# 16-dim attention heads in one block: projection, stacking, scores, exp times V, sums and output, with a lag of two head pairs

## The reference, cut to what matters

```
q, k, v = split into 16 heads of 16 features of   xq @ Wq, xk @ Wk, xk @ Wv
sim     = q @ k^T * scale          (causal: only keys up to the query)
e       = exp(sim - max over keys of sim)
out     = (e @ v) / (sum over keys of e)
x       = x + concat(out) @ Wo
```

## Time and profile before

| | |
|---|---|
| median of 3 runs | 4298.7 us (4296.89 to 4308.47) |
| the profiled execution | 4299.54 us, span 4297.7 us from first to last instruction |
| TensorE busy | 3401.4 us, 79% of the span |
| VectorE busy | 2078.9 us, 48% |
| ScalarE busy | 1146.9 us, 27% |
| mean granted TensorE clock | 0.888 of full speed |
| 12 executions of the three blocks | first at 93.7 us, last ends at 4162.7 us |

### The profile page before, as it was taken

How to read it: one execution, slowest core, us unless ns; L and a number is a source line. 1 busy time by engine, 2 the same in 40 slices (tenths; PEclk the granted TensorE clock), 3 DMA queues, 4 the chain that set the end, 5 groups by cost and what they waited for, 6 DMA issues and landing times. The chain is left out here.

```text
span 4297.7 us, 49457 instructions
## 1 busy us (share of the span) xinstructions
PE 3401.4 (79%) x18289; PEld 2170.2 (50%) x18289; DVE 2078.9 (48%) x4553; ACT 1146.9 (27%) x2199; POOL 401.3 (9%) x381
## 2 busy tenths in 40 slices
PE   4778689678869967887986778798595888877888
PEld 3364555436455544645454455544593454454545
DVE  3655445465545546555555654554113435344353
ACT  1413125141223414122341312243131213112121
POOL 0010101010010101001010100101102000010100
PEclk9888899888889978898997979899797998989989
DMA  4000100200010010001001000100682110102011
GB/s 163 13 13 21 63 11 1 86 13 13 21 63 11 17 70 13 13 20 63 11 28 59 13 13 23 61 10 33 246 306 97 51 41 7 78 8 84 8 51 38
DMA packets 53212, 209.27 MB, mean 49 GB/s; under 512 B 4977, under 2 KB 37617, under 8 KB 41329
## 3 DMA queue, kind: packets, MB, share of 16 engines
q1 hardware_dynamic: 48128, 198.85, 12.5%
q0 software_dynamic: 1536, 4.20, 0.3%
q10 hardware_dynamic: 3312, 3.02, 0.2%
HBM read 186.89 MB, written 19.16 MB: 48 GB/s over the span
## 5 line engine op out<-in xcount | busy, mean ns | idle before, releaser
L643 DVE TENSOR_REDUCE nmax<-psum 128x1 f32<-128x512 f32 (+3 forms) x768 | 392.2, 553 | 135.6 <-PE psum L579 91.5
L685 ACT ACTIVATE probs<-psum 128x1024 f32<-128x1024 f32 (+3 forms) x384 | 304.4, 814 | 431.0 <-PE psum L607 290.0
L108 PE MATMUL psum<-select 128*128 128x512 f32 x1016 | 280.2, 431 | 82.9 <-PEq L120 82.9
L574 PE MATMUL psum<-ks,qs 64*128 64x512 f32 (+3 forms) x768 | 211.1, 546 | 139.5 <-DVE nmax L643 123.5
L108 PEld LDWEIGHTS psum<-select 128*128 128x128 f32 x1016 | 205.3, 208 | 156.9 <-issue 113.3
L316 ACT ACTIVATE xc<-psum 128x256 f32<-128x256 f32 x152 | 54.5, 389 | 790.1 <-PE psum L309 790.1
L265 POOL TENSOR_SCALAR rstd<-mean_var 128x4 f32<-128x4 f32 x48 | 10.9, 228 | 2491.5 <-DVE mean_var L290 2491.5
L574 PEld LDWEIGHTS psum<-ks,qs 64*128 64x128 f32 x768 | 89.0, 227 | 290.2 <-DVE nmax L643 269.5
L1490 ACT ACTIVATE exps<-exps,nmax 128x512 f32<-128x512 f32 x256 | 183.4, 717 | 71.4 <-DVE nmax L1436 71.0
L1436 DVE CUSTOM_DVE_ANT_0 exps<-psum,mrows 128x512 f32<-128x512 f32 x256 | 166.1, 689 | 67.9 <-PE psum L1383 64.6
L602 PE MATMUL psum<-qs,ks 64*128 64x512 f32 (+3 forms) x768 | 165.0, 435 | 7.8 <-ACT probs L685 7.8
(11 more groups left out here) (371 smaller groups left out, 6700.9 us busy)
## 6 DMA issues: line engine op xcount, KB each, us to landing
arena<-in_w SPq DMA_DIRECT2D x23, 1028.0 KB, 5.0
arena<-in_w SPq DMA_DIRECT2D x23, 1024.0 KB, 5.2
arena<-in_pack_L_ffn SPq DMA_DIRECT2D x4, 5184.5 KB, 15.5
arena<-in_pack_L_xattn SPq DMA_DIRECT2D x4, 4744.0 KB, 13.9
arena<-in_pack_L_ffn SPq DMA_DIRECT2D x4, 4120.0 KB, 13.1
arena<-in_pack_L_attn SPq DMA_DIRECT2D x5, 2432.0 KB, 9.2
arena<-in_pack_L_attn SPq DMA_DIRECT2D x9, 1280.0 KB, 5.5
arena<-ternary SPq DMA_DIRECT2D x4, 2056.0 KB, 7.8
```

The source lines that it names most:

```text
L108: pe.matmul(self.psum[:, bank, :], self.select[:, 0, :], self.select[:, 0:BANK // P, :], start=True, stop=True)
L574: mm = pe.matmul(net.psum[:, bank_of(s + j), 0:w], qs[half, p, qt * P:(qt + 1) * P], ks[half, p, 0:w], start=True, stop=not causal)
L643: dve.tensor_reduce(nmax[:, p, qt, n % 2:n % 2 + 1], net.psum[:, bank_of(s), 0:w], AX.X, ALU.max, negate=True).then_inc(row_read, 1)
L685: act.activation(probs[:, n % buffers, :, lo:T], net.psum[:, first:first + 2, lo:T], ACT.Exp, scale=scale)\
```

## The change

`stack_pairs` and `heads_of_four` are gone; `softmax_heads` is one block that also does the division and output of its sublayer.

- TensorE: the projections come first, then the stacking of pairs 0 and 1, then the score steps. The stacking of pairs 2 to 7 and the four value products stand between the score steps of pairs 0 and 1.
- ScalarE copies both q and k of the stacked pairs (k with ones as a bias) and all values; VectorE copies none of them any more.
- The lag is two pairs in place of three. Each pair's exp is done for all four key tiles in turn, so a `weigh`, which needs both pairs of a group, comes in four steps in a row and then not for four steps; the even pair's exp is kept in four tiles, the odd pair's in two.
- The division goes by groups of four heads: `totals` (four products with 4 columns) puts the sums on query rows, VectorE takes a reciprocal of 128x16 and widens it to 128x512, `spread_inverse` turns it back, VectorE scales o in place, `project` adds to the output. Groups 0 to 2 stand in the last eight steps beside the last exps, group 3 comes at the end.
- Semaphores per block 28 in place of 20. No DMA is added, removed or moved.

```diff
-SEMS = 20
+SEMS = 28
...
+    lag, steps = 2, NT
+    ring = (0, 1, 2)
...
+                def stack(p):
+                    for is_k in range(2):
+                        m, src = 2 * p + is_k, 2 * (p // 4) + is_k
+                        pe.wait_ge(high_done, src + 1)
+                        pe.wait_ge(low_done, max(src, min(m, 3)) + 1)
+                        if m >= 4:
+                            pe.wait_ge(stacked, m - 3)
...
+                def values(t):
+                    if t:
+                        pe.wait_ge(v_copied, t)
...
                 def row_scores(p, qt):
 
+                    if qt == 0:
+                        pe.wait_ge(stacked, 2 * p + 2)
...
                 def col_scores(n):
+                    p, kt = divmod(n, steps)
+                    if kt == 0:
+                        pe.wait_ge(row_read, put_slot(p) + 1)
                     if n >= 2:
                         pe.wait_ge(probs_done, n - 1)
+                    else:
+                        pe.wait_ge(stacked, outputs)
...
+                def totals(g):
+                    pe.wait_ge(o_done, g + 1)
+                    if g:
+                        pe.wait_ge(scaled, g)
+                    else:
+                        pe.wait_ge(row_read, turns)
+                    for t in range(NT):
+                        mm = pe.matmul(net.psum[:, 0, 4 * t:4 * t + 4], o[:, g, t * P:(t + 1) * P], net.gather[:, 0:PITCH:8],
+                                       start=True, stop=True)
+                    mm.then_inc(totals_done, 1)
+
+                def spread_inverse(g):
+                    pe.wait_ge(widened, g + 1)
...
+                def project(g):
+                    pe.wait_ge(scaled, g + 1)
...
+                stack(0)
+                stack(1)
                 for p in range(PAIRS + lag):
                     for i in range(steps):
                         if p < PAIRS:
                             row_scores(p, i)
+                        if p < 2:
+                            if i % 2 == 0:
+                                stack(2 + 3 * p + i // 2)
+                            else:
+                                values(2 * p + i // 2)
+                            if i == 3:
+                                stack(4 + 3 * p)
                         if p >= lag:
                             n = (p - lag) * steps + i
                             col_scores(n)
-                            if n % 2 and n >= 3:
-                                weigh((n - 3) // 2)
+                            last_p, last_kt = divmod(n - 1, steps)
+                            if n and last_p % 2:
+                                weigh(last_p // 2, last_kt)
                         if 1 <= p <= PAIRS and i == (PUT_AT // 2 - 1 if p < PAIRS else 0):
                             put(p - 1)
+                        if p >= PAIRS:
+                            at = (p - PAIRS) * steps + i
+                            if at in (1, 3, 5):
+                                totals(at // 2)
+                            if at in (2, 4, 6):
+                                spread_inverse(at // 2 - 1)
+                            if at in (3, 5, 7):
+                                project(at // 2 - 1)
+                weigh(GROUPS - 1, steps - 1)
+                totals(GROUPS - 1)
+                spread_inverse(GROUPS - 1)
+                project(GROUPS - 1)
...
+                        act.activation((ks if is_k else qs)[:, p, :], net.psum[:, 3 + m % 4, :], ACT.Identity, **bias).then_inc(stacked, 1)
...
+                    dve.reciprocal(inverse[:, g % 2, :, :], net.psum[:, 0, 0:NT * 4].rearrange("p (t h) -> p t h", t=NT)).then_inc(inverse_done, 1)
```

More of the change, by code:

```diff
@@ L530, in heads_of_four, with jobs @@
-def heads_of_four(net, qs, ks, v, o, scale, guard=None, causal=False):
-    lag, buffers = 3, 4
-    steps, units = NT, PAIRS // 2
-    tiles = 2 * NT
-    ring = (0, 1, 7)
     halves = [slice(j * STACK, (j + 1) * STACK) for j in range(2)]
+    if jobs is None:
+        def jobs(j, c):
+            return chunk_terms(*((W["wk"], ksrc) if j else (W["wq"], qsrc)), c), None
+    table = [jobs(j, c) for c in range(NC) for j in range(2)]
     def slot(p, n):
@@ L553, in heads_of_four @@
         with net.block() as (block, sem):
+            product_done, value_done, high_done, low_done = sem("product"), sem("value"), sem("high"), sem("low")
+            cos_done, sin_done, zeroed = sem("times cosine"), sem("times sine"), sem("zeroed")
+            placed, stacked = sem("parts in place"), sem("stacked q or k copied")
+            v_done, v_copied = sem("values product"), sem("values copied")
             cleared, scores_done = sem("spread zeroed"), sem("a tile's scores, both heads")
@@ L561, in _ @@
+            widened = sem("1/sum of a group, for each partition of a head")
+            spread_done, scaled, out_done = sem("1/sum on the heads' partitions"), sem("group scaled"), sem("output of a tile")
             @block.gpsimd
@@ new lines, in _ @@
+                for n, groups in enumerate(table):
+                    if rope and n >= 2:
+                        pe.wait_ge(sin_done, n - 1)
+                    for which, group in enumerate(groups):
+                        for where, lhsT, rhs, start, stop, turn in group or ():
+                            mm = pe.matmul(net.psum[:, job_bank(n, which), :], lhsT, rhs, start=start, stop=stop)
+                    mm.then_inc(product_done, 1)
+                stack(0)
+                stack(1)
@@ new lines, in _ @@
+                for n in range(len(table)):
+                    act.wait_ge(value_done if rope else product_done, n + 1)
+                    act.activation(high[:, n, :], source(n), ACT.Identity).then_inc(high_done, 1)
+                copy_stack(0)
+                copy_stack(1)
+                for p in range(2):
+                    for i in range(steps):
+                        if i % 2 == 0:
+                            copy_stack(2 + 3 * p + i // 2)
+                        else:
+                            copy_values(2 * p + i // 2)
+                        if i == 3:
+                            copy_stack(4 + 3 * p)
@@ new lines, in _ @@
+                for n in range(PAIRS * steps):
+                    p, kt = divmod(n, steps)
+                    lo = kt * P if causal else 0
+                    act.wait_ge(colscores_done, n + 1)
+                    if p % 2 and kt >= 2:
+                        act.wait_ge(pv_done, p // 2 * steps + kt - 1)
+                    if p >= 2:
+                        act.wait_ge(pv_done, (p // 2 - 1) * steps + (kt + 1 if p % 2 == 0 else steps))
+                    first = 3 + 2 * (n % 2)
+                    act.activation(probs(n)[:, :, lo:T], net.psum[:, first:first + 2, lo:T], ACT.Exp, scale=scale).then_inc(probs_done, 1)
```

229 lines of the change are left out of this document (91 added, 138 removed).

## The result

The change makes the kernel 0.7% faster: 4268.14 us in the median of 4 runs (4267.12 to 4270.88), before 4297.8 beside it; ratio 0.9931, 95% interval 0.9914 to 0.9948. The gain is 30 us where 164 were forecast; 4268 lies far outside the range of 4088 to 4212.

A forecast was written before the change was run, and what follows sets the result against it. No engine fills the span; each stage has its own bound, with VectorE busy 47.6 of 54.1 us in L0_xattn's rows. Gains of 13.8, 11.8 and 15.6 us, four times each, make 165: 4134 us, range 4088 to 4212.

The forecast's parts named there:

- three signs of being wrong: Row scores in pairs 0 and 1 wait for stacked copies; clock in pairs 2 to 7 below 0.9; a tail longer.
- Part 1, the head: First product to first maximum: gains of 10.5 us in L0_xattn, 10.3 in L1_attn, 14.1 in L3_attn per execution.
- Part 2, the rows: First to last maximum: L0_xattn gains 2.1 us less 2.0 for one clock fall, net 0.1; causal rows gain 0.
- A stack: Rows, pairs 0 and 1: a stacking product is four TensorE passes at 0.22 us, 0.9 in all.
- a value tile: Rows, pairs 0 and 1: a value product costs TensorE 0.86 us.
- the 2.0 taken: L0_xattn rows: price in us of one clock fall, counted in the middle steps of pair 2.
- The rival of falls in every even pair: L0_xattn rows: three clock falls of 2.0 us per execution, 72 less the 8 counted, 4198 us; chance 0.15.
- the same count gives less than 1 us either way: Causal rows: mask products fill the steps, so gain taken as 0, bounds 2 us up and down.
- Part 3, the tail: Last maximum to last add: 27.7 us against 30.9 in L0_xattn, gain 3.2; causal 26.3 against 27.8, gain 1.5.
- TensorE's queue to 19.2 us: L0_xattn tail: 2.3 to the add, 15.9 of queued TensorE products, 1.0 of uncovered VectorE answers.
- The serial end: L0_xattn tail, after 19.2 us: last group's product, copy, totals, reciprocal, spread, scaling, project and adds, ending at 27.7.
- my rivals: Falls in every even pair 4198 us (0.15); stacking waits 4242 (0.10); slower 4418 (0.03); better about 4100 (0.10).

The follow-up runs named there:

- the run with the old division: The changed kernel with division and output done by the block of before, after the block; head, rows and lag of two pairs stay: 4204.5 us.
- the old order: The kernel before with only its head changed, so order, lag of three pairs and division as before: 4189.6 us, 4190.6 in a second set.
- experiment 6: Two kernels with new head and division of before: order of before with lag three, 4189.6 us; the change's order with lag three, 4283.9 us.
- Run 3: The changed kernel with output products of groups 0 to 2 moved behind the last product of exp and v: 4205.7 us.
- Run 2: The changed kernel plus unread products in the tail: two ahead of each of the last eight column scores, sixteen at the end: 4262.4 us.
- experiment 7: Changed kernel with division of before and lag two, plus either values ahead of stacking, 4245.3 us, or two unread products before each of the last eight column scores, 4224.1.
- experiment 4: The changed kernel with late output products, plus two unread products ahead of each of the last eight column scores: 4203.2 us.
- the old order with late output: Order of before in the rows behind the new head, division by groups in the block, all output products late: 4172.6 us against 4297.8 before.

## Why the prediction was wrong

The sign was right and the size was not. Of the three signs of being wrong the last came true: the causal tails are longer than before. Of the 133 us that are missing (165 against 32 in the span), 71 are the tails, 36 the rows, 14 the code outside and 11 the heads.

**Part 1, the head: right but for the clock.** 12.6, 9.8 and 21.3 us were measured in the mean, 11.4, 9.9 and 19.5 forecast. The two that are longer than forecast have a clock below 1.00 in them (0.76 in the first L0_xattn, 0.93 in the last L3_attn). In the run with the old division two L3_attn heads stand at 1.00 and take 20.1.

**Part 2, the rows: two terms too small, one left out.** In the first L1_attn's pair 1, with TensorE's queue full:

```profile
330.61 0.50 PE L505 MATMUL psum<-high,select 128*128 128x512 f32 x1
...
331.75 0.38 PE L526 MATMUL psum<-ks,qs 64*128 64x256 f32 x2
...
332.19 1.13 PE L513 MATMUL psum<-arena,xc 128*128 128x256 f32 x4
...
333.25 0.44 PE L526 MATMUL psum<-ks,qs 64*128 64x384 f32 x2
```

A stack takes 1.14 from start to next start (330.61 to 331.75; forecast 0.9), a value tile 1.06 (332.19 to 333.25; forecast 0.86). In L0_xattn pairs 0 and 1 take 6.48 and 7.63 (5.95 and 6.6 forecast); the odd pairs' 6.97 and even pairs' 6.33 are close to 6.9 and 6.15. One pair in each L0_xattn holds a fall: 8.33 in place of 6.97, a price of 1.4 against the 2.0 taken. That it is one, as counted, is luck: it was counted in the middle steps of pair 2, and it comes in pair 5 or 7, among the products of exp and v. The rival of falls in every even pair, with the rule of the Trainium skill ("TensorE: Matmul & The Clock Gate", "psum-queue depth-cycling") beside it, did not come about in the rows. What failed is the sentence that in the causal rows "the same count gives less than 1 us either way". Maxima are shorter there (VectorE busy 34.6 of 51.1), so the stacks, values and bunched products are not beside anything longer. Pairs 0 and 1 take 13.7 from the first maximum, where before they took 11.5 to 12.1. Pairs 5 and 6 of the first L1_attn, the change ahead and the old order of experiment 6 behind:

```profile
356.00:362.69 6.69, 6.33 (x78) 3.16 (x76) 4.41 (x11) 2.82 (x4) 0.00 (x0) 1.00 0.01 2
362.69:368.07 5.38, 4.35 (x62) 2.85 (x60) 4.41 (x11) 3.29 (x5) 0.00 (x0) 1.00 0.00 0
```

```profile
353.42:358.96 5.54, 5.11 (x64) 2.65 (x62) 4.41 (x11) 4.14 (x5) 0.00 (x0) 1.00 0.01 4
358.96:364.93 5.97, 5.52 (x76) 3.31 (x76) 4.50 (x11) 1.96 (x4) 0.00 (x0) 1.00 0.00 0
```

At full clock and with the same work (TensorE busy 10.7 and 10.6 us in the two pairs) the bunched order takes 12.07 and the old one 11.51: TensorE fills the odd pair and has 1.0 us to spare in the even one. Behind the new head the old order takes back 22 of the rows' 36 us (experiment 6).

**Part 3, the tail: the clock taken as full, one product misplaced.** For L0_xattn I summed TensorE's queue to 19.2 us up to the last exp; it came at 19.1. The agreement is partly luck: the sum holds a third output product (1.73) and a third product of exp and v (1.0), which TensorE ran behind the last column scores (181.17), and leaves out the 1.56 us from these scores to the end of the last exp and 0.1 of each column score and spread. The serial end, forecast at 8.45, took 11.6:

```profile
181.17 0.50 PE L554 MATMUL psum<-qs,ks 64*128 64x512 f32 x2
...
181.71 1.02 ACT L745 ACTIVATE probs_odd<-psum 128x1024 f32<-128x1024 f32 x1 [1.49 <-PE psum L554]
...
182.59 1.99 PE L599 MATMUL psum<-arena,o 128*128 128x256 f32 x8
184.52 0.62 PE L573 MATMUL psum<-probs_even,v 128*32 128x512 f32 x2
...
190.11 3.45 PE L599 MATMUL psum<-arena,o 128*128 128x256 f32 x8 [0.78 <-DVE o L699]
```

The last exp ends at 182.73, but its product with v waits to 184.52 behind the output product of group 2: 1.8. The last output product runs at 1.2 GHz, 3.45 for 1.95: 1.5. Run 3 undoes the first and finds 26.7 us at full clock, 1.0 under my 27.7. In the causal tails, forecast at 26.3, nearly all of the miss is the clock. Run 2 at full clock and in the change's own order has 31.1 with 32 products too many. The sixteen in the first half are worth 2.9 (experiment 7), the sixteen at the end 1.1: what follows the last exp takes 10.8 with them, and 9.7 in the change's second L3_attn tail, whose end stands at 1.00. So some 27 would be left (an estimate), 7 less than L1_attn's 34.3 and close to the forecast. The order is 3.5 of these 27 (experiment 4), but that cost was in the forecast's queue too. The two are not independent: run 3 has the first fall where it was in all causal tails, but not the second, and no fall in three of the four L0_xattn tails. The step that failed is the clock, which Part 3 took at full speed throughout. That it could fall in the tail was in none of my rivals; I looked for falls in the rows alone, because the tail before stood at 1.00.

**Outside.** The code outside the twelve executions took 3049.0 us of the span before, 3062.9 after, and 3052 to 3064 in the profiles of the other runs. Two of the 14 us are seen ahead of the first L0_xattn, which starts at 95.6 us in place of 93.7, with a fall of the clock from 71.0 us on that the trace of before has not. Another 11 lie in the three stretches from the end of an L1_attn to the next L0_xattn, which took 419.4, 416.7 and 415.9 us before and 421.3, 421.0 and 420.9 after, with mean clocks of 0.91 to 0.92 and 0.90. What sets such falls in stages that the change doesn't touch was not tried and stays open.

## What to carry over

Before moving work beside other work, ask of each stage which engine sets its pace: beside VectorE's long maxima two thirds of the values' cost were hidden, beside the shorter causal ones half. In an in-order queue, put nothing that is needed only at the end ahead of what another engine waits for; moving three groups of output products behind the last product of exp and v was worth 62 us and costs no work; at full clock on both sides it brings the last exp 3.4 to 3.5 us sooner in each execution, and the rest came with the clock. And where a change puts other products into a stretch that stood at full clock, count a fall there, not only in the stretches that had one: TensorE was as busy in the new causal tail as in the old (30.1 of 34.3 us against 24.1 of 27.8), and the clock fell all the same.

## What the runs showed of the chip that I had not expected

- Four products (eight passes) with 4 columns take 1.05 us, four with 128 columns 1.16, at 1.2 GHz 1.84 and 1.86 (totals and spreads in the tails): a product of 4 columns costs about as much as one of 128.
- Two heads' product of exp and v costs what four heads' cost, 0.98 against 1.00 us.
- The clock in the tail goes with the order of the products ahead of it and in it: 1.00 in all twelve tails with the order of before (three kernels: the kernel before, the old order, and the old order with late output) and with two heads in every step and the old division (0.89 to 0.94 with the division by groups); 0.73 to 1.00 where four steps hold a product of exp and v and the next four none, unless products are added. Which feature of the order decides was not taken apart further.
- The same code costs 26.7 us at clock 1.00 and 31.0 at 0.83 (L0_xattn's tail in run 3).
